# Values' products two steps behind the exponentials, and PSUM banks split 4 to 3 between ScalarE's and VectorE's rings, in the attention half of a fused float32 kernel

## What is computed

```python
def _L1_attn_ref(x, ln_scale, ln_bias, wq, wk, wv):   # 16 heads of 8
    xn = _layernorm(x, ln_scale, ln_bias)
    q, k, v = (heads(xn @ w) for w in (wq, wk, wv))
    scores = jnp.einsum('bhid,bhjd->bhij', q, k)
    probs = jax.nn.softmax(scores / jnp.sqrt(jnp.float32(128)), axis=-1)
    out = jnp.einsum('bhij,bhjd->bhid', probs, v)
    return out.transpose(0, 2, 1, 3).reshape(bs, sl, -1) + xn

x = x + _L1_attn_ref(_layernorm(x), ...)
x = x + 0.5 * (relu(_layernorm(x) @ w1 + b1) @ w2 + b2)
```

## Time and profile before

| | us |
|---|---|
| median of 3 runs | 2095.85 (2092.15 to 2098.02) |
| the profiled execution | 2089.9 |
| its span, first to last instruction | 2087.8 |

### The profile page before, as it was taken

The page is one execution under the profiler, slowest core; times in us unless marked ns, Lnnn a source line. Parts: engine busy times, 40 slices in busy tenths (PEclk is TensorE's granted clock), DMA queues, the critical chain, the costliest instruction groups (busy, mean ns, idle before and its releaser), DMA issues. The chain is left out here.

```text
span 2087.8 us, 34428 instructions
## 1 busy us (share of the span) xinstructions
PE 1933.9 (93%) x12468; PEld 1335.6 (64%) x12468; DVE 1537.2 (74%) x3852; ACT 1174.1 (56%) x2215; POOL 670.3 (32%) x767
## 2 busy tenths in 40 slices
PE   3999999999999999999999478999999999999997
PEld 2888888888888888888888323444444444444443
DVE  5767686666767677676776168888888888888881
ACT  3444444444444444444443137888887888878874
POOL 2333343234333343333431212333333333333311
PEclk9999999999999999999999659999999999999998
DMA  3000000000000000000000122222222222222210
GB/s 125 6 11 11 1 11 11 11 1 11 11 11 11 1 11 11 11 11 1 11 6 6 36 78 90 84 85 85 86 82 79 85 85 85 79 81 85 80 47 11
DMA packets 49992, 85.81 MB, mean 41 GB/s; under 512 B 6752, under 2 KB 11104, under 8 KB 49760
## 3 DMA queue, kind: packets, MB, share of 16 engines
q1 hardware_dynamic: 47920, 81.85, 12.5%
q10 hardware_dynamic: 1904, 1.78, 0.3%
HBM read 49.26 MB, written 34.87 MB: 40 GB/s over the span
## 5 line engine op out<-in xcount | busy, mean ns | idle before, releaser
L1344 DVE TENSOR_REDUCE b_nm<-b_MX 128x1 f32<-128x512 f32 x1024 | 649.6, 683 | 101.8 <-PE b_MX L1459 93.7
L1235 ACT ACTIVATE b_pr<-b_ST 128x512 f32<-128x512 f32 x1024 | 550.1, 601 | 153.6 <-PE b_ST L1446 151.1
L410 ACT ACTIVATE s<-G 128x512 f32<-128x512 f32 x306 | 182.7, 597 | 350.9 <-PE G L714 348.2
L1459 PE MATMUL b_MX<-b_kt,b_qt 32*128 32x512 f32 x1024 | 350.4, 505 | 22.1 <-DMA b_qt<-staging 11.6
L719 PE MATMUL Y<-w_wd,h 128*128 128x128 f32 x2448 | 329.0, 277 | 17.4 <-DVE h L575 16.1
L1446 PEld LDWEIGHTS b_ST<-b_qt,b_kt 32*128 32x128 f32 x1024 | 126.7, 183 | 320.4 <-ACT b_pr L1235 209.8
L1446 PE MATMUL b_ST<-b_qt,b_kt 32*128 32x512 f32 x1024 | 313.1, 497 | 19.8 <-ACT b_pr L1235 18.7
L566 DVE TENSOR_TENSOR su<-U,s 128x512 f32<-128x512 f32 x272 | 187.0, 687 | 190.6 <-PE U L714 113.5
L719 PEld LDWEIGHTS Y<-w_wd,h 128*128 128x128 f32 x2448 | 305.8, 192 | 33.2 <-DVE h L575 23.9
L1474 PE MATMUL b_PV<-b_pr,b_va 128*32 128x512 f32 x2048 | 276.2, 612 | 0.0
L575 DVE TENSOR_TENSOR h<-C,su 128x512 f32<-128x512 f32 x272 | 188.0, 691 | 9.3
(11 more groups left out here) (246 smaller groups left out, 3492.4 us busy)
## 6 DMA issues: line engine op xcount, KB each, us to landing
b_kt<-staging SPq DMA_DIRECT2D x64, 256.0 KB, 2.8
b_qt<-staging SPq DMA_DIRECT2D x64, 256.0 KB, 3.4
staging<-b_khi SPq DMA_DIRECT2D x32, 256.0 KB, 3.0
staging<-b_qhi SPq DMA_DIRECT2D x32, 256.0 KB, 3.2
xin<-in_x SPq DMA_DIRECT2D x17, 256.0 KB, 2.9
mid<-xo SPq DMA_DIRECT2D x17, 256.0 KB, 2.0
b_x<-mid SPq DMA_DIRECT2D x16, 256.0 KB, 3.1
staging<-b_klo SPq DMA_DIRECT2D x16, 256.0 KB, 3.1
```

The lines of the kernel that those rows point to most:

```text
L410: nc.scalar.activation(sbuf_s[n % 2][:], G[n % 2][:], ACT.Silu).then_inc(act_done.sem, 1)
L1235: nc.scalar.activation(pr[k % 2][:, j], bank[:].rearrange("p a b -> p (a b)"), ACT.Exp, scale=SM_SCALE).then_inc(used["st"].sem, 1)
L1344: nc.vector.tensor_reduce(nm[g % 2][:, c:c + 1], bank[:].rearrange("p a b -> p (a b)"), AX.X, ALU.max).then_inc(used["mx"].sem, 1)
L1459: pe.matmul(flat(MX[place % MX_BANKS]), qt[g][rows_of(j), u // HG % T], flat(kt_[g])[rows_of(j)], start=True, stop=True).then_inc(made["mx ...
```

## The change

```diff
+LAG = 2
-ST_BANKS, MX_BANKS = 3, 4
+ST_BANKS, MX_BANKS = 4, 3
 SMALL = [
-    [], [("nm", 0, 1), ("ot", -1, 3)], [], [("xt", 1, 0)],
+    [], [("nm", 0, 1)], [("ot", -1, 3)], [("xt", 1, 0)],
     [("kp", 1, 0)], [("nm", 0, 2), ("qp", 1, 0)], [("ot", 0, 0)], [("v", 1, 0)],
-    [("ft", -1, 0)], [("nm", 0, 3), ("ot", 0, 1)], [("g", -1, 0)], [("g", -1, 1)],
+    [("ft", -1, 0)], [("nm", 0, 3)], [("ot", 0, 1), ("g", -1, 0)], [("g", -1, 1)],
     [("g", -1, 2)], [("nm", 1, 0), ("g", -1, 3)], [("ot", 0, 2), ("y", -1, 0)], [("y", -1, 1)]]
-        pr = [sb(f"pr{k}", [P, HG, N]) for k in range(2)]
+        pr = [sb(f"pr{k}", [P, HG, N]) for k in range(LAG + 1)]
+        def weights_of(B, k):
+            return pr[(B.number * STEPS + k) % (LAG + 1)]
 # ScalarE, exponential(B, k, j)
-                if j == 0 and (k >= 2 or not B.first):
-                    act.wait_ge(pv_mm.sem, B.at(pv_mm, k - 1))
+                if j == 0 and (k > LAG or not B.first):
+                    act.wait_ge(pv_mm.sem, B.at(pv_mm, k - LAG))
-                nc.scalar.activation(pr[k % 2][:, j], ...
+                nc.scalar.activation(weights_of(B, k)[:, j], ...
 # ScalarE, batch_steps: where PV is copied out
-                        if j == 1 and k == 0:
+                        if j == 2 and k == LAG - 1:
                             weights_out(B + -1, GRP - 1)
-                        elif j == 1 and k % T == 0:
+                        elif j == 2 and k % T == LAG - 1:
                             weights_out(B, k // T - 1)
 # VectorE, side: the second layernorm's statistics
-                if prv.exists and k in (3, 4, 5):
+                if prv.exists and k in (4, 5, 6):
 # TensorE, batch_steps
-                        if j == 1 and k == 0:
-                            weighted(B + -1, STEPS - 1)
+                        if j == 1 and k < LAG:
+                            weighted(B + -1, STEPS - LAG + k)
                         elif j == 1:
-                            weighted(B, k - 1)
+                            weighted(B, k - LAG)
```

More of the change, by code:

```diff
@@ L1230, in exponential @@
                 act.wait_ge(made["st"].sem, B.at(made["st"], u + 1))
-                if j == 0 and (k >= 2 or not B.first):
-                    act.wait_ge(pv_mm.sem, B.at(pv_mm, k - 1))
+                if j == 0 and (k > LAG or not B.first):
+                    act.wait_ge(pv_mm.sem, B.at(pv_mm, k - LAG))
                 bank = ST[ST_PLACE["st", 0, u] % ST_BANKS]
-                nc.scalar.activation(pr[k % 2][:, j], bank[:].rearrange("p a b -> p (a b)"),
+                nc.scalar.activation(weights_of(B, k)[:, j], bank[:].rearrange("p a b -> p (a b)"),
                                      ACT.Exp, scale=SM_SCALE).then_inc(used["st"].sem, 1)
@@ L1319, in side @@
                         total("1")
-                if prv.exists and k in (3, 4, 5):
-                    if k == 3:
+                if prv.exists and k in (4, 5, 6):
+                    if k == 4:
                         dve.wait_ge(xf_ready.sem, prv.at(xf_ready, 1))
@@ L1324, in side @@
                             dve.wait_ge(mv_ready["f"].sem, prv.at(mv_ready["f"], 0))
-                    if k < 5:
-                        stats("f", xf, (0, 1) if k == 3 else (2, 3))
+                    if k < 6:
+                        stats("f", xf, (0, 1) if k == 4 else (2, 3))
                     else:
@@ L1473, in weighted @@
                 for j in range(HG):
-                    mm = pe.matmul(flat(PV)[rows_of(j)], va[B.parity][:, kt, g * HG + j], pr[k % 2][:, j],
+                    mm = pe.matmul(flat(PV)[rows_of(j)], va[B.parity][:, kt, g * HG + j], weights_of(B, k)[:, j],
                                    start=(kt == 0), stop=(kt == T - 1), skip_group_check=True)
```

## The result

The changed kernel takes 2130.61 us (median of 4 runs, 2128.96 to 2132.32) against 2094.32 us before (4 runs, 2092.15 to 2098.02). The ratio is 1.0172, 95% interval 1.0153 to 1.0190: slower by 36 us. Its profiled execution took 2132.32 us, its span is 2130.5; between the two profiled executions the difference is 42 us, 6 more than between the medians. The forecast was 2125 us, with a range from 2110 to 2138.

What follows compares the result with a forecast made beforehand. Loops of waits through several engines bound the kernel, no engine alone. Fourteen batches +29.5, first +2, last +2.1, transfers -2.5: +31 us on 2089.9 gives 2121, or 2127 from the median; taken 2125, 80% range 2110 to 2138.

Steps and rivals of the forecast that it cites:

- Loop A: `MX` 1 of the next step waits for VectorE's maximum 3, making 3.33 us between blocks of values' products.
- the `ot` in steps 2 and 10: Steps now holding `ot` in VectorE's three-bank ring go to 3.33 us: +0.67 in step 2, +0.23 in step 10.
- The gains: Steps 0, 11, 12 and 15 get shorter by 0.02, 0.33, 0.44 and 0.58 us, 1.37 a batch together.
- step 5: Step with `nm` and `qp`: `qp` goes 2.31 us after the block's start, so the step takes 3.60, +0.27.
- the moved `PV` copy costs 0: On ScalarE, the copy behind exponential 2 never waits and its 0.49 us finds room in steps of 3.3.
- The strips' waits at step 8: `MX` 0 waits for the next batch's strips in 4 of 15 batches; more slack saves 0 to 3.8 us, taken -2.5.
- The first batch: About +1 us from step 5 on, 0 to +1.5 in slow steps 1 to 4; taken as +2.
- The last batch: Steps 1 to 8 lose 2.5 us, steps 9 to 15 gain about 1.4, one extra block costs 1.00: +2.1.
- Faster, the wait hides: At the next step's `MX` 1, the wait for maximum 3 hides fully, leaving only gains: -20 us, 2075; chance 5%.
- no change: Only half the steps with one small product fall into Loop A, so losses equal gains: 2096 us; chance 4%.
- The clock's rival: TensorE's idling drops its granted clock to 0.50 for one batch: some 15 us, 2140 and more; chance 4%.
- The rival of ScalarE and the transfers: ScalarE or the transfers become late, at most +0.5 us a batch for each of two bounds: +15, 2140; chance 7%.

Runs made afterwards that it cites:

- half maxima: The changed kernel with each row maximum taken over 256 of the 512 columns: 2048.51 us against 2091.66 for the kernel before.
- the banks alone: The kernel before with only the rings' banks changed (ScalarE 4, VectorE 3), lag 1 and old list of small work: 2110.98 us against 2092.83.
- the lag with running rings: The changed kernel with ScalarE 3 banks, VectorE 4, and rings going on over batches instead of restarting at bank 0: 2085.3 us, ratio 0.9956 to the kernel before.
- the version with two `ot` moved and 4 banks: The kernel before, rings continuing over batches, two `ot` moved to steps 2 and 10, statistics one step later; VectorE 4 banks: 2068.6 us against 2095.21.
- the kernel before with running rings: The kernel before, changed only so each ring's next batch continues where the last ended, not at bank 0: 2083.46 us, ratio 0.9962.

## Why the prediction was right, and where it was off

*The mechanism* was right for what costs the time. Loop A, read from three steps of the old trace, sets steps 1, 2, 3, 6, 8, 9 and 10 of the new one at 3.33 or 3.34 each. The half maxima confirm it by changing its length; the banks alone confirm what lets it in.

*The split of the cost.* Of the 2.55 a batch, 1.41 come with the banks (51.65 to 53.06), 1.15 with the two moved `ot` (to 54.21), 0.0 with the lag. The prediction had the `ot` in steps 2 and 10 as part of the banks' price (+0.67 and +0.23), which is the same sum; that the move is harmful only with three banks, and a gain with four, it did not say.

*The gains* came as forecast: steps 11 and 12 at 2.76, step 15 at 3.89, step 0 at 2.73. TensorE's idle time for exponentials is nearly gone, 2.3 us of 18.7. The prediction gave the lag a share in this, and it has next to none: without it steps 11, 12, 15 and 0 take 2.76, 2.93, 3.90 and 2.76, and the 0.17 more in step 12 stand against 0.13 less in step 13.

*The terms that were mis-sized*, together 0.45 a batch: step 13 (+0.14) and step 4 (+0.08), where VectorE's own work of maxima and statistics starts the second pair late; step 5 (+0.12), of which 0.08 is the wait for the `nm` copy behind the moved `PV` copy (without the lag it takes 3.64); step 14 (+0.07) and step 15 (+0.04), where `y` takes 1.98 from its start to the next `ST` 0 in place of 1.93. Step 7 was 0.06 less; the rest are hundredths. Over fourteen batches this is 6 us. The statement that the moved `PV` copy costs 0 was wrong in principle: it looked at whether the copy itself waits, and for the maxima's way back at steps 1 and 9 alone, but the copy delays what ScalarE does behind it, in step 5 above all. In the changed kernel this costs 0.08 a batch; with ScalarE's ring of three the lag costs 0.68.

*The ends and transfers.* The strips' waits at step 8 went altogether (-3.8, taken as -2.5). The first batch's T(2) came 2.2 later and its length from there grew by 1.1: +3.3 where +2 was taken. The last batch took 6.7 more from T(2) to the block that was the last before, where 1.1 was forecast, and the one block more took 0.9 (forecast 1.0). Of the 6.7, 5.5 go with the clock, which stood at 0.58 from 2067 to 2071 and at 0.63 on average from 2078 to 2092, with 1.00 between:

```profile
2067.00:2071.00 4.00, 4.00 (x22) 1.49 (x20) 2.72 (x9) 1.92 (x4) 2.10 (x3) 0.58 0.02 6
...
2078.00:2092.00 14.00, 13.43 (x50) 4.82 (x50) 0.55 (x2) 9.16 (x19) 2.50 (x2) 0.63 0.00 1
```

Step 6 took 4.29 there against 3.33 in the batches before it, and steps 10 to 12 took 13.15 against 8.63 in the kernel with the half maxima, which is the same kernel in these steps. Before, steps 9 to 15 of the last batch ran at 1.00. Such dips also stand in the first or last batches of other traces of this case (the lag with running rings, for one). None stands in the fourteen batches between in before or after, but the version with two `ot` moved and 4 banks has one there, and steps 9 to 11 of that batch took 13.12 in place of 9.19:

```profile
1565.00:1575.00 10.00, 10.00 (x47) 4.09 (x47) 6.04 (x11) 5.60 (x12) 0.11 (x1) 0.59 0.00 1
```

TensorE was busy throughout these ten us. Whether the longer loop made the dip of the changed kernel is open. Summed: 14 x 2.55 = 35.7, + 3.3, + 6.7, + 0.9, - 3.8 is 42.8, against 42.7 between the two spans.

*The number.* The sum was made for the profiled execution, +31 us to 2121, and that came out at +42, 2132: 6 us from the steps and 5.5 from the clock are missing, and the rest of the ends and the transfers cancel. Taking 2125, towards the median of the runs shown, and the medians' difference of 36 brought forecast and result within 6 us; that part is luck.

*The rivals.* "Faster, the wait hides" and "no change" did not happen in any of the step intervals. The clock's rival happened for 18 us of one batch, at 5.5 of the 42 us between the profiled executions, and not in the middle. The rival of ScalarE and the transfers did not happen here, but did with four banks for VectorE: there the lag makes step 7 of every batch wait for the maxima's transfer.

## What to carry to other kernels

With engines in a fixed order, write down for each step the loop of waits that closes it (product, reader, bank free, next product) and count which earlier place in the ring a product waits for: a bank taken away moves every wait one place nearer, and its price here was one maximum (0.60) in each step where that place moved from maximum 2 to maximum 3. Giving the bank to ScalarE's ring gained in the steps with a `g` and lost more in VectorE's. That a longer lag adds no instruction does not make it free: what moves with it in an engine's fixed order, here the copy of `PV`, delays everything behind it, up to transfers that another engine issues in order. Whether it pays to spread small products over more steps depends on the ring's depth (-0.79 a batch at four banks, +1.15 at three). A ring that starts again each batch should have a length divisible by its banks, or run on. And name a run by all that it changes: a gain of 0.79 and a cost of 0.68 in one run read as "no effect".

## What the runs showed that was not expected

A long block of products is not only an obstacle: placed between two pairs of products it shares out the time in which the readers get nothing. Moved next to the small work it cost 82 us in the changed kernel (2130.61 to 2212.52) and 126 us in the kernel before with running rings (2083.46 to 2209.5). The start-to-start distance of back-to-back maxima is not fixed: 0.60 in pairs, and (2.62 - 0.69) / 3 = 0.64 in the run of four shown for step 4.
